# Four places of a fused graph network kernel: layer norm coefficients shared between VectorE and GpSimd, an earlier bank signal, and another order at the end of the score stage

## The chip, the cores and the metric

One NeuronCore of a Trainium2 chip runs the whole program in a single launch. The metric is the device time of that launch in microseconds. Engines are named as the profile names them: PE (TensorE), DVE (VectorE), ACT (ScalarE), POOL (GpSimd) and SP (the queue that issues most DMAs).

## The reference, cut to what matters

The input x has 128 graphs of 128 nodes with 128 features. Four blocks follow one another, each of the form x = x + block(relu(layernorm(x))):

```python
h = jnp.maximum(_layernorm(x, axis=-1), 0.0)
x = x + L0(h, W, adj, bias)                  # diagonal, upper and lower part of adj, each with its own W
h = jnp.maximum(_layernorm(x, axis=-1), 0.0)
x = x + L1(h, adj, ...)                      # GCN: A_hat h W1 + b1, batchnorm, relu, W2 + b2, batchnorm
h = jnp.maximum(_layernorm(x, axis=-1), 0.0)
x = x + L2(h, adj, ...)                      # two graph convolutions, then LSTMs over windows of 1 to 4 nodes
h = jnp.maximum(_layernorm(x, axis=-1), 0.0)
x = x + L3(h, src, dst, ...)                 # attention over 256 edges: scores, softmax per source node, sum
```

All arithmetic is fp32, or fp32 split into a high and a low part for the faster pass of PE.

## The kernel before, in words

X stays in SBUF as 32 tiles of 4 graphs (128 partitions by 512 elements). Each stage runs over the tiles in 16 turns of two slots, s = 0 and 1. The program is written engine by engine, and every engine's order is the order of its instructions; semaphores tie the engines together. There are no planner and no due times around the change: an engine that waits holds back all that is written behind the wait.

**Layer norm coefficients.** DVE makes statistics of a tile with four `bn_stats` (`LayerNormTail.stats`, L126). Then POOL turns the six statistics of each graph into 1/std (`rstd`) and -mean/std (`nmr`) in five dependent groups (`batch`, L153 to L179): sum, difference, squares, a `pow` with exponent -0.5, and two products. It does so for both slots of a turn at once (128x8 operands). Only for the very first turn of the first stage it goes tile by tile (`coefficients_alone`, 128x4). ACT waits for these (`LayerNormTail.wait`) and normalises a tile with four activations (`normalise_tile`, L185).

**First stage** (`stage_first`). DVE's order at the start is: statistics of tile 0, the split of the adjacency, a copy of its diagonal, statistics of tile 1, the row sums (`degrees`), a memset, statistics of tiles 2 and 3 interleaved with the low parts of h for tiles 0 and 1 (`h_low`, L468), then the loop over turns. PE transposes h (L410), multiplies with the adjacency (L418 to L420, which wait for `h_low`) and then with the weights (L431 to L433). Dummy matmuls (`stay_awake`, L80) keep PE busy before that.

**GCN out part** (`stage_gcn_out`). DVE makes the batchnorm coefficients (L703 to L713), then four products for the signed projection (L783 to L789) and three for the value projection (L796 to L801), and after them gives the free signal of the two PSUM banks (`O_stored`, L807). ACT makes h2 from the coefficients (L755), and PE (L772, L774) waits for h2 and for the bank signal. In the loop DVE takes each tile out of the bank (L813) and makes statistics of it (L816).

**Convolution stage** (`stage_conv`). A step t does work for several tiles at once: the residual of tile t+4 (PE turns it over, L854; DVE adds it to X, L861, and makes its statistics, L126), the normalised tile t+1 on ACT, the products of tiles t to t-3 on PE (L979, L1002), each taken over by DVE (L1029, L1025, L1019) or ACT (L971, L962). The steps t = -4 to -1 are the head of the stage. `FILL` gives numbers of dummy matmuls in some steps. POOL makes the coefficients for two tiles at a time.

**Scores** (`Scores`, last turns i = 13, 14 and 15). Per turn PE transposes h (L1528), makes Q (L1541), V (L1547) and, from q split by ACT (L1503) and DVE (L1580), the edge sums (L1560, L1561). DVE makes M from these (L1593), POOL halves it (L1450), DVE sums it (L1459). The softmax of the first chunk of scores is spread over the last turns: `score_in` to `subtract_max` on DVE at the end of turn 13 (L1657 to L1670), the exponential on ACT in turn 14 in front of the normalisation of tile (15,0) (L1674), `turn_back` on PE between the two V products of turn 14 (L1684), `keep_exponential` on DVE (L1689), `sum_up` on PE in front of the edge sums of turn 14 (L1695), `invert` (L1701) and `weigh` (L1705) on DVE. The exponential's table is loaded at the end of turn 13 (L1679). `at.high`, `at.low`, `at.gather` and `at.weighted` (L1799, L1803, L1758, L1836) are the first steps of the attend stage behind it.

## Time and profile before

| | us |
|---|---|
| median of 3 runs | 1208.47 (1206.82 to 1209.98) |
| the profiled execution | 1208.81 |
| its span | 1207.0 |
| PE busy in the span | 1175.3 (97%) |
| DVE busy | 978.5 (81%) |
| ACT busy | 899.6 (75%) |
| POOL busy | 438.3 (36%) |

The span runs from the first to the last instruction of the core; 1.81 us of the execution lie outside it. PE is nearly always busy, so the time is read from the places where PE waits, or where its granted clock is lower than full: the timeline of each engine in such a stretch tells what was late, and the chain of work that ended last tells whether the wait was on the path. In a timeline the first column is the start in us, the second the duration from the first to the last of the instructions merged into the row, then engine, line, operation, output and inputs, and in brackets the engine's idle time before it and what ended it.

### The profile page before, as it was taken

How to read it: one execution, taken by the hardware profiler on the slowest of the kernel's cores; microseconds unless marked ns; L12 is line 12 of the kernel's file. 1: busy time of each engine (PE TensorE's matmuls, PEld its weight loads, DVE VectorE, ACT ScalarE, POOL GpSimd, SP SyncE). 2: the span in 40 equal slices, each digit the busy share in tenths (PEclk: the TensorE clock that was granted, in tenths of full speed). 3: DMA queues.
4: the chain of work that ended last, by engine and by line, in shares of the span. 5: the costliest groups of instructions: out<-in, count | busy, mean ns of one | idle time of the engine just before them, and what ended most of it. 6: DMA issues, size and time to landing. Idle time of an engine off the chain costs nothing.

```text
span 1207.0 us, 22297 instructions
## 1 busy us (share of the span) xinstructions
PE 1175.3 (97%) x7208; PEld 1018.0 (84%) x7208; DVE 978.5 (81%) x2005; ACT 899.6 (75%) x1729; POOL 438.3 (36%) x803
## 2 busy tenths in 40 slices
PE   8999999999999999999999999999999999989998
PEld 8999988864688886798878887898898899978997
DVE  5888859978788877988788878887787799978774
ACT  5767669968588878877787868776776688875554
POOL 5778747800277450000000000000000477757764
PEclk9999999999999999999999999999999999999999
DMA  8000000000311100000000000000300120001122
GB/s 326 1 2 2 2 1 0 1 1 0 113 71 63 67 36 1 1 2 1 1 1 1 2 0 2 1 1 1 140 2 1 37 105 2 2 1 53 70 76 82
DMA packets 14923, 38.21 MB, mean 32 GB/s; under 512 B 1904, under 2 KB 3952, under 8 KB 13808
## 3 DMA queue, kind: packets, MB, share of 16 engines
q1 hardware_dynamic: 14000, 36.60, 7.9%
q8 instruction: 50, 0.82, 0.3%
q10 hardware_dynamic: 832, 0.46, 0.1%
q14 instruction: 41, 0.34, 0.1%
HBM read 20.27 MB, written 16.78 MB: 31 GB/s over the span
## 4 chain that ended last, share of the span: by engine, by line
PE 67%; DVE 6%; ACT 3%; issue 1%; POOL 1%; POOLq 0%; DVEq 0%; ACTq 0%
PE psum L1241 7%; PE psum L979 7%; PE psum L1242 7%; PE psum L1240 7%; PE psum L1269 5%; PE psum L1265 4%; PE psum L1266 4%; PE psum L1541 2%; PE psum L1793 2%; PE psum L772 2%; PE psum L774 2%; PE psum L1758 2%; PE psum L1547 2%; PE psum L1002 2%; PE psum L1768 2%; ACT gates L1286 2%
## 5 line engine op out<-in xcount | busy, mean ns | idle before, releaser
L1286 ACT ACTIVATE gates<-psum,lstm_bias 128x512 f32<-128x512 f32 (+1 forms) x504 | 302.2, 637 | 99.2 <-PE psum L1269 86.9
L153 POOL TENSOR_TENSOR l2r_sum<-l2r_st 128x8 f32<-128x8 f32 x16 | 5.2, 322 | 500.8 <-DVE l2r_st L126 500.5
L185 ACT ACTIVATE l_h<-X,nmr,rstd 128x128 f32<-128x128 f32 (+1 forms) x392 | 160.6, 484 | 14.3 <-POOLq L179 14.3
L1241 PE MATMUL psum<-lstm_node_hi,Wih_lo 128*128 128x512 f32 (+1 forms) x408 | 148.3, 363 | 0.0
L1242 PE MATMUL psum<-lstm_node_lo,Wih_hi 128*128 128x512 f32 (+1 forms) x408 | 148.0, 363 | 0.0
L1240 PE MATMUL psum<-lstm_node_hi,Wih_hi 128*128 128x512 f32 (+1 forms) x408 | 148.0, 363 | 0.0
L1265 PE MATMUL psum<-lstm_hid_hi,Whh_hi 128*128 128x512 f32 (+1 forms) x288 | 104.1, 361 | 3.9 <-DVE lstm_hid_hi L1348 3.7
L1269 PE MATMUL psum<-lstm_hid_lo,Whh_hi 128*128 128x512 f32 (+1 forms) x288 | 107.3, 373 | 0.0
L1266 PE MATMUL psum<-lstm_hid_hi,Whh_lo 128*128 128x512 f32 (+1 forms) x288 | 103.0, 358 | 0.0
L1296 ACT ACTIVATE gates<-lstm_cell 128x512 f32<-128x512 f32 (+1 forms) x144 | 83.7, 581 | 20.9 <-DVE lstm_cell L1335 20.5
L1240 PEld LDWEIGHTS psum<-lstm_node_hi,Wih_hi 128*128 128x128 f32 x408 | 77.2, 189 | 10.8 <-ACT gates L1286 0.3
L1242 PEld LDWEIGHTS psum<-lstm_node_lo,Wih_hi 128*128 128x128 f32 x408 | 77.2, 189 | 10.2
L1241 PEld LDWEIGHTS psum<-lstm_node_hi,Wih_lo 128*128 128x128 f32 x408 | 77.2, 189 | 10.1
L1329 DVE TENSOR_TENSOR lstm_cell<-gates 128x512 f32<-128x512 f32 (+1 forms) x72 | 46.9, 651 | 30.1 <-ACT gates L1286 27.6
L1269 PEld LDWEIGHTS psum<-lstm_hid_lo,Whh_hi 128*128 128x128 f32 x288 | 54.1, 188 | 16.0 <-DVE lstm_hid_lo L1350 10.2
L1265 PEld LDWEIGHTS psum<-lstm_hid_hi,Whh_hi 128*128 128x128 f32 x288 | 54.2, 188 | 12.1 <-DVE lstm_hid_hi L1348 6.1
L1331 DVE TENSOR_TENSOR gates<-gates 128x512 f32<-128x512 f32 (+1 forms) x72 | 43.8, 608 | 25.1 <-ACT gates L1286 24.8
L1266 PEld LDWEIGHTS psum<-lstm_hid_hi,Whh_lo 128*128 128x128 f32 x288 | 54.4, 189 | 6.8
L1343 DVE TENSOR_TENSOR Y<-gates 128x512 f32<-128x512 f32 (+1 forms) x72 | 46.5, 646 | 13.7 <-ACT gates L1296 13.7
L755 ACT ACTIVATE l1b_h<-Y,l1b_coef 128x512 f32 (+1 forms) x64 | 48.5, 806 | 11.2 <-PE psum L774 9.1
L431 PE MATMUL psum<-W,l_z 128*128 128x128 f32 x256 | 50.3, 278 | 3.6 <-DVE l_z L540 3.0
L340 ACT ACTIVATE l_z<-psum 128x512 f32<-128x512 f32 x32 | 19.1, 597 | 42.3 <-PE psum L420 42.3
(279 smaller groups left out, 3449.7 us busy)
## 6 DMA issues: line engine op xcount, KB each, us to landing
x_spill<-X SPq DMA_DIRECT2D x32, 256.0 KB, 2.0
X<-x_spill SPq DMA_DIRECT2D x2, 4096.0 KB, 12.9
out<-X SPq DMA_DIRECT2D x32, 256.0 KB, 2.0
X<-in_x SPq DMA_DIRECT2D x6, 1024.0 KB, 15.3
X<-in_x SPq DMA_DIRECT2D x3, 512.0 KB, 7.8
w_raw<-in_WihT SPq DMA_DIRECT2D x1, 1024.0 KB, 5.3
w_raw<-in_WhhT SPq DMA_DIRECT2D x1, 1024.0 KB, 7.6
X<-in_x SPq DMA_DIRECT2D x2, 256.0 KB, 3.5
```

Of the source, the lines that this page charges most:

```text
L185: last = act.activation(h[:, j, :], k.X[:, bass.ds(b0, TB), :][:, j, :], ACT.Relu, bias=k.nmr[:, bass.ds(b0, TB)][:, j:j + 1], scale=k.rst ...
L431: pe.matmul(o, Z0[s][:, j, :], W0[:, 0, :], start=True, stop=False)
L755: act.activation(h2[s][:, c, :], Y[c][:, bass.ds((i * S + s) * TW, TW)], ACT.Relu, bias=coef[:, c, 1:2], scale=coef[:, c, 0:1]).then_inc(h ...
L979: last = pe.matmul(ps[:, j * P:(j + 1) * P], lhs[:, j, :], rhs, start=True, stop=True)
L1240: pe.matmul(out, hi, x_high, start=True, stop=False)
L1241: pe.matmul(out, lo, x_high, start=False, stop=False)
L1242: last = pe.matmul(out, hi, x_low, start=False, stop=it.step == 0)
L1265: pe.matmul(out, hi, h_high, start=False, stop=False)
L1266: pe.matmul(out, lo, h_high, start=False, stop=False)
L1269: pe.matmul(out, hi, h_low, start=False, stop=True).then_inc(done[s], 1)
L1286: act.activation(gate_of(it, g), k.bank[4 * s + g][:, 0:it.N], ACT.Tanh if g == GATE_G else ACT.Sigmoid, bias=k.lstm_bias[:, it.p - 1, g:g ...
L1296: act.activation(gate_of(it, GATE_G), cell[it.slot][:, 0:it.N], ACT.Tanh).then_inc(tanh_ready[it.slot], 1)
```

## The change

1. Layer norm coefficients of the first two turns, in the first stage (`x_ln`) and at the head of the convolution stage (the residual's `ln`), are made by DVE and POOL together: `aggregate` on DVE (a `bn_aggr` for each graph, and + EPS), `root` on POOL (the `pow` alone), `shift` on DVE (-mean * rstd). The first turn goes tile by tile, the second both tiles at once. Later turns are made as before.
2. In the GCN out part the bank signal stands ahead of the coefficients and the projections.
3. In the convolution stage the numbers of dummy matmuls in the head change, and DVE makes the residual update behind the other work in steps 0 to 2.
4. In the last turns of the scores the softmax steps move to later places, and the normalisation of tile (15,1) goes from ACT to POOL.

```diff
+    def aggregate(self, dve, turn, s=0):
+        before, first, width, _ = self.shared_rows(turn, s)
+        for slot in [s] if turn == 0 else range(self.S):
+            dve.wait_ge(self.stats_ready[slot], turn + 1)
+        dve.sem_inc(self.dve_tally, 1)
+        for j in range(width):
+            last = dve.bn_aggr(self.mv[:, j, :], self.st6[:, first + j:first + j + 1, :])
+        last.then_inc(self.quick, 1)
+        dve.wait_ge(self.quick, before + 1)
+        if turn or s == self.S - 1:
+            dve.sem_inc(self.stats_free[0], 1)
+        dve.tensor_scalar(self.mv[:, 0:width, 1], self.mv[:, 0:width, 1], EPS, None, ALU.add).then_inc(self.quick, 1)
+
+    def root(self, pool, turn, s=0):
+        before, _, width, rows = self.shared_rows(turn, s)
+        pool.wait_ge(self.quick, before + 2)
+        pool.tensor_tensor(out=self.k.rstd[:, rows], in0=self.mv[:, 0:width, 1], in1=self.k.ln_const["-half"][:, 0:width],
+                           op=ALU.pow).then_inc(self.quick, 1)
+
+    def shift(self, dve, turn, s=0):
+        before, _, width, rows = self.shared_rows(turn, s)
+        dve.wait_ge(self.quick, before + 3)
+        dve.scalar_tensor_tensor(self.k.nmr[:, rows], self.mv[:, 0:width, 0], -1.0, self.k.rstd[:, rows],
+                                 ALU.mult, ALU.mult).then_inc(self.quick, 1)
+        dve.wait_ge(self.quick, before + 4)
+        dve.sem_inc(self.ready[0], 1)
...
             x_stats(0, [0])
+            x_ln.aggregate(dve, 0, 0)
             dve.wait_ge(masks, 2)
...
             dve.tensor_copy(diag_bc[:, :], spare[:, 0:P]).then_inc(diag_done, 1)
+            x_ln.shift(dve, 0, 0)
             x_stats(0, [1])
+            x_ln.aggregate(dve, 0, 1)
             degrees()
+            x_ln.shift(dve, 0, 1)
+            h_low(0, 0)
+            x_stats(1)
+            x_ln.aggregate(dve, 1)
+            h_low(0, 1)
             dve.memset(cont[:, :], 0.0).then_inc(cleared, 1)
-            x_stats(1, [0])
-            h_low(0, 0)
-            x_stats(1, [1])
-            h_low(0, 1)
...
+                if i == 0:
+                    x_ln.shift(dve, 1)
                 if i + AHEAD < n_it:
                     x_stats(i + AHEAD)
...
+        for s in range(S):
+            dve.sem_inc(O_stored[s], 1)
         coef_dve(dve)
         signed_projection()
         value_projection()
-        for s in range(S):
-            dve.sem_inc(O_stored[s], 1)
...
-    FILL = {-2: 3, -1: 4, 0: 18, 1: 1}
+    FILL = {-2: 5, -1: 6, 1: 3}
...
+        def first_coefficients(dve, t):
+            ln = res.ln
+            if 0 < t <= S:
+                ln.shift(dve, 0, t - 1)
+            if 0 <= t < S:
+                ln.aggregate(dve, 0, t)
+            if t == 2 * S - 1:
+                ln.aggregate(dve, 1)
...
-            if there(t + RES):
+            late = isinstance(t, int) and 0 <= t < 3
+            if there(t + RES) and not late:
                 res.update(dve, i + RES // S, [s])
+            if isinstance(t, int) and t < 0:
+                first_coefficients(dve, t + RES)
...
                 dve.tensor_copy(Z[:, :, :], as_tile(psZ)).then_inc(Z_done, 1)
+            if there(t + RES) and late:
+                res.update(dve, i + RES // S, [s])
+            if isinstance(t, int) and t == 0:
+                res.ln.shift(dve, 1)
...
+    def normalise_on_pool(self, pool, i, s):
+        k, h = self.k, self.h[s]
+        self.ln.wait(pool, s, i)
+        pool.wait_ge(self.R["Tp"][s], i)
+        for j in range(TB):
+            b = (i * self.S + s) * TB + j
+            last = pool.tensor_scalar(h[:, j, :], k.X[:, b, :], k.rstd[:, b:b + 1], k.nmr[:, b:b + 1], ALU.mult, ALU.add)
+        last.then_inc(self.normed, 1)
+        pool.wait_ge(self.normed, 1)
+        pool.tensor_scalar(h[:, :, :], h[:, :, :], 0.0, 0.0, ALU.max, ALU.add).then_inc(self.R["h"][s], 1)
...
                 if i == n_it - 1 and s == 0:
                     at.low(pool, 2)
+            if i == n_it - 3:
+                self.normalise_on_pool(pool, n_it - 1, 1)
...
-            if i == n_it - 2:
-                at.sm.exponential(act, 0)
+            if i == n_it - 1:
+                for t in range(2):
+                    at.high(act, t)
...
-            if i + 1 < n_it:
+            if i + 2 < n_it:
                 self.normalise(act, i + 1, 1)
-            if i == n_it - 3:
+            if i == n_it - 2:
                 at.sm.load_exponential(act)
-            if i == n_it - 2:
-                for t in range(2):
-                    at.high(act, t)
+                at.sm.exponential(act, 0)
...
+            if i == n_it - 1:
+                at.sm.turn_back(pe, 0)
...
-                if i == n_it - 2 and s == S - 1:
-                    at.sm.turn_back(pe, 0)
+                if i == n_it - 1 and s == 0:
+                    at.sm.sum_up(pe, 0)
...
-            if i == n_it - 2:
-                at.sm.sum_up(pe, 0)
...
-            if i and i != n_it - 2:
+            if i and i < n_it - 2:
                 self.sum_heads(dve, i - 1)
...
-            if i == n_it - 2:
-                at.sm.keep_exponential(dve, 0)
+            if i == n_it - 1:
+                at.sm.invert(dve, 0)
+                at.sm.weigh(dve, 0)
+            if i >= n_it - 2:
                 self.sum_heads(dve, i - 1)
-                at.sm.invert(dve, 0)
...
             if i == n_it - 2:
-                at.sm.weigh(dve, 0)
+                at.sm.keep_exponential(dve, 0)
```

In the last turns this gives the following orders. DVE, turn 14: low parts of q, `sum_heads` of turn 13, M, `keep_exponential`; turn 15: low parts of q, `invert`, `weigh`, `sum_heads` of turn 14, M of slot 0, `weighted(0)`, M of slot 1, `weighted(1)`. ACT, turn 14: both hT, normalisation of (15,0), q, V, table load, exponential; turn 15: both hT, `high(0)`, `high(1)`, q, V. PE, turn 15: both transposes, `turn_back`, Q, `sum_up`, V, edge sums. POOL: the normalisation of (15,1) stands behind the halving of turn 13, and ahead of that of turn 14.

## Rows read from the trace of the kernel before

**Rows 1.** The page: its first line, and the chain that ended last by engine
```profile
span 1207.0 us, 22297 instructions
...
PE 67%; DVE 6%; ACT 3%; issue 1%; POOL 1%; POOLq 0%; DVEq 0%; ACTq 0%
```

**Rows 2.** Timeline of the first stage's start, 0 to 40 us, several engines
```profile
5.38 0.86 DVE L126 BATCH_NORM_STATS2 x_st<-X 128x6 f32<-128x128 f32 x4
...
8.49 1.07 POOL L153 TENSOR_TENSOR x_m<-x_m,ln_const 128x4 f32<-128x4 f32 x1 [0.18 <-POOL x_m L153]
...
9.89 0.20 POOL L153 TENSOR_TENSOR nmr<-x_sum,x_m 128x4 f32<-128x4 f32 x1
10.17 1.65 ACT L185 ACTIVATE l_h<-X,nmr,rstd 128x128 f32<-128x128 f32 x4 [6.17 <-POOLq L179]
...
16.28 0.69 DVE L468 TENSOR_TENSOR l_h_lo<-l_h,l_h_hi 128x512 fp32r<-128x512 f32 x1 [2.29 <-ACT l_h_hi L325]
...
17.03 0.19 PEld L418 LDWEIGHTS psum<-l_A_hi,l_h_hi 128*128 128x128 f32 x1 [0.25 <-DVE l_h_lo L468]
```

**Rows 3.** Timeline of DVE at the head of the out part: small instructions
```profile
253.47 0.15 DVE L705 TENSOR_SCALAR bn_mv<-bn_mv 128x1 f32<-128x1 f32 x1
253.54 1.01 DVE L703 BATCH_NORM_AGGREGATE bn_mv<-bn 128x2 f32<-128x192 f32 x1
```

**Rows 4.** Head of the out part: timelines of ACT and PE, and one window
```profile
255.31 2.93 ACT L755 ACTIVATE l1b_h<-Y,l1b_coef 128x512 f32<-128x512 f32 x4 [2.09 <-DVE l1b_coef L713]
...
257.79 1.20 PE L772 MATMUL psum<-l1b_h,W2T 128*128 128x512 f32 x2 [2.41 <-DVEq L807]
...
263.02 1.02 PE L772 MATMUL psum<-l1b_h,W2T 128*128 128x512 f32 x2
...
260.00:262.00 2.00, 2.00 (x3) 0.67 (x2) 0.90 (x2) 1.16 (x2) 0.00 (x0) 0.50 0.00 0
```

**Rows 5.** Timelines at the head of the convolution stage: DVE, ACT, POOL, PE
```profile
323.18 0.87 DVE L126 BATCH_NORM_STATS2 l1r_st<-X 128x6 f32<-128x128 f32 x4 [0.18 <-DVE X L861]
...
328.51 1.65 ACT L185 ACTIVATE l_h<-X,nmr,rstd 128x128 f32<-128x128 f32 x4 [5.49 <-POOLq L179]
...
330.72 1.65 POOL L153 TENSOR_TENSOR l1r_m<-l1r_m,ln_const 128x8 f32<-128x8 f32 x1 [0.18 <-POOL l1r_m L153]
...
333.05 1.65 ACT L185 ACTIVATE l_h<-X,nmr,rstd 128x128 f32<-128x128 f32 x4
...
335.27 1.16 PE L979 MATMUL psum<-Wg,l_G 128*128 128x128 f32 x8 [0.67 <-ACT l_G L971]
```

**Rows 6.** Timelines of the last turns of the scores: ACT, PE and DVE
```profile
1064.95 1.28 ACT L1679 ACT_TABLE_LOAD   x1
1066.25 0.20 ACT L1679 ACTIVATE sm_unread<-zero 128x1 f32<-128x1 f32 x1
...
1066.99 2.05 PE L1541 MATMUL psum<-Wqv,l_hT 128*128 128x128 f32 x16 [1.32 <-ACT l_hT L1496]
...
1068.81 0.42 DVE L1670 TENSOR_TENSOR sm_r<-sm_r,sm_w 128x256 f32<-128x256 f32 x1
...
1073.41 1.16 PE L1695 MATMUL psum<-scores,same 128*128 128x128 f32 x8 [2.33 <-DVE scores L1689]
...
1077.31 0.63 PE L1561 MATMUL psum<-l_q_lo,PT 128*128 128x512 f32 x1
...
1074.61 1.76 DVE L1701 RECIPROCAL sm_m<-psum 128x256 f32<-128x256 f32 x1
...
1076.28 2.42 DVE L1593 SCALAR_TENSOR_TENSOR l_M<-psum,a_sign 128x512 f32<-128x512 f32 x4
...
1087.80 1.28 DVE L1836 TENSOR_TENSOR at_w<-psum,scores 128x512 f32<-128x512 f32 x2
```

**Rows 7.** Groups by line and shape, POOL: busy time and mean of one
```profile
L609 POOL TENSOR_SCALAR l_h<-l_h 128x256 f32<-128x256 f32 x26 | 27.8, 1068 | 5.4 <-POOL l_h L604 5.4
...
L604 POOL TENSOR_SCALAR l_h<-X,rstd,nmr 128x128 f32<-128x128 f32 x52 | 23.0, 453 | 9.0 <-PE psum L659 6.9
```

More of the change, by code:

```diff
@@ L88, with __init__ @@
     GROUPS = 5
-    def __init__(self, k, ctx, name, S, nb=TB, per=2, at=None, first_alone=False, places=1):
-        self.first_alone, self.places = first_alone, places
+    def __init__(self, k, ctx, name, S, nb=TB, per=2, at=None, first_alone=False, places=1, shared=0):
+        self.first_alone, self.places, self.shared = first_alone, places, shared
         top = at
@@ L106, in __init__ @@
         self.stats_free, self.ready = (each(S // per, lambda q: k.sem(f"{name}_{n}{q}")) for n in ("stfree", "coef"))
+        if shared:
+            self.mv = place("mv", [P, per * nb, 2])
+            self.quick = k.sem(f"{name}_quick")
         self.step, self.tally, self.dve_tally = (k.sem(f"{name}_{n}") for n in ("step", "tally", "dve_tally"))
@@ L116, in wait @@
     def wait(self, eng, s, turn):
-        eng.wait_ge(self.ready[s // self.per], turn + 1 + (self.first_alone and (turn > 0 or s == 1)))
+        eng.wait_ge(self.ready[s // self.per], turn + 1 + (self.first_alone and (not isinstance(turn, int) or turn > 0 or s == 1)))
     def stats(self, dve, xt, s, turn):
@@ L127, in stats, with shared_rows @@
         last.then_inc(self.stats_ready[s], 1)
+    def shared_rows(self, turn, s):
+        n = s if turn == 0 else turn + 1
+        first, width = (s * self.nb, self.nb) if turn == 0 else (0, self.per * self.nb)
+        return 4 * n, first, width, slice(turn * self.per * self.nb + first, turn * self.per * self.nb + first + width)
+    def aggregate(self, dve, turn, s=0):
[22 more added lines that the diff above has]
+        dve.sem_inc(self.ready[0], 1)
     def coefficients(self, pool, turn):
@@ L147, in batch @@
         late = self.first_alone and (alone is None or alone == 1)
-        base = (turn * self.batches + q + late) * self.GROUPS
+        base = (turn * self.batches + q + late - (self.shared and self.shared + 1)) * self.GROUPS
         rows = bass.ds((turn * self.batches + q) * whole + first, width)
@@ L252, in stage_first @@
     spare = psO[0]
-    x_ln, ln = LayerNormTail(k, ctx, "x", S, first_alone=True), k.l0_ln
+    x_ln, ln = LayerNormTail(k, ctx, "x", S, first_alone=True, shared=2), k.l0_ln
     SCALE, SPREAD, READ, KEYS, WIDE, RANK, PERM, SORTED, ROUND, ADJ, SUM, TURN, SHARE = 0, 2, 2, 3, 4, 5, 6, 8, 9, 10, 11, 12, 13
@@ L295, in _ @@
             for s in range(S):
-                x_ln.coefficients_alone(pool, s)
+                x_ln.root(pool, 0, s)
             pool.wait_ge(deg, 4)
             pool.tensor_tensor(out=dinv[:, :], in0=rs[:, 3:4], in1=k.ln_const["-half"][:, 0:1], op=ALU.pow).then_inc(dinv_p, 1)
-            x_ln.coefficients(pool, 1)
+            x_ln.root(pool, 1)
             pool.iota(order_row[:, :], [[1, E]], base=0, channel_multiplier=0, allow_small_or_imprecise_dtypes=True).then_inc(iotas, 1)
@@ L737, in stage_gcn_out @@
     tally, logged, signed = hidden.tally, sem("l1b_logged"), sem("l1b_signed")
-    joined, stats_done = sem("l1b_joined"), sem("l1b_stats")
+    stats_done = sem("l1b_stats")
     unread = sb("l1b_unread", [P, 1])
@@ L795, in value_projection @@
             dve.wait_ge(signed, 4)
-            dve.tensor_tensor(W[:, 0:P], e.Wqv[:, 0:P], e.a_sign[:, :], ALU.mult).then_inc(joined, 1)
-            dve.wait_ge(joined, 1)
+            dve.tensor_tensor(W[:, 0:P], e.Wqv[:, 0:P], e.a_sign[:, :], ALU.mult).then_inc(signed, 1)
+            dve.wait_ge(signed, 5)
             dve.tensor_reduce(W[:, P:P + H], W[:, 0:P].rearrange("p (x d) -> p x d", x=H), mybir.AxisListType.X,
-                              ALU.add).then_inc(joined, 1)
-            dve.wait_ge(joined, 2)
-            dve.tensor_copy(W[:, 0:P], e.Wqv[:, P:2 * P]).then_inc(joined, 1)
+                              ALU.add).then_inc(signed, 1)
+            dve.wait_ge(signed, 6)
+            dve.tensor_copy(W[:, 0:P], e.Wqv[:, P:2 * P]).then_inc(signed, 1)
+        for s in range(S):
+            dve.sem_inc(O_stored[s], 1)
         coef_dve(dve)
@@ L843, in __init__ @@
         self.o_ready, self.R_ready, self.updated = (each(S, lambda s: k.sem(f"{name}_{n}{s}")) for n in ("o", "R", "upd"))
-        self.ln = LayerNormTail(k, ctx, name, S)
+        self.ln = LayerNormTail(k, ctx, name, S, first_alone=True, shared=2)
     def fetch(self, act, s, source):
@@ L927, in on_pool @@
         AHEAD = 2
-        for i in range(AHEAD):
-            res.coefficients(pool, i)
+        for s in range(S):
+            res.ln.root(pool, 0, s)
+        res.ln.root(pool, 1)
         for n, W in enumerate((k.Wih, k.Whh)):
@@ L1407, in __init__ @@
         self.R = {n: each(S, lambda s: k.sem(f"l3_{n}{s}")) for n in names}
+        self.normed = k.sem("l3_normed")
         self.n_it = k.B // TB // S
```

## The prediction

> **What bounds the kernel now.** I read the chain of work that ended last first: PE holds 67% of the span on it [rows 1], so a saving counts where PE waits for something late, or runs at a low clock. The changed lines lie in four such places, each read from the engines' timelines.
>
> *Start.* POOL's last product starts at 9.89, ACT normalises tile 0 at 10.17, though its statistics began at 5.38 [rows 2]. PE starts the products of tile 1 at 17.03, released by `h_low`, which ran from 16.28 [rows 2].
>
> *Out part.* ACT begins h2 at 255.31, PE only at 257.79, after 2.41 us of waiting for the bank signal behind DVE's projections [rows 4]. Its granted clock then falls to 0.50 (1.2 of 2.4 GHz) between 260 and 262 [rows 4]; the third tile starts at 263.02.
>
> *Convolution head.* ACT gets its first coefficients at 328.51 and those of turn 1 for 333.05; PE enters its steady order at 335.27, released by ACT's G [rows 5].
>
> *Score end.* PE waits 1.32 us for hT, which stands behind the table load, and 2.33 us at `sum_up`; after that each edge pass takes 0.63 us, at a lower clock [rows 6].
>
> **The change, part by part.** Times are those of the profiled execution.
>
> *Small instructions on DVE.* No row shows a `bn_aggr` of six numbers. Two small DVE instructions without a dependence started 0.07 us apart [rows 3]; the aggregate of 192 numbers took 1.01 us [rows 3]; a `bn_stats` of 128 took 0.20 per instruction (0.87 for four, the last with its latency [rows 5]). If the 1.01 is a fixed 0.15 [rows 3] and the rest by length, six numbers add 0.03. I take 0.10 each; the ends are 0.07 and, should the price be all fixed, 1.0. One `aggregate` of four then takes about 0.15 (wait and semaphore, as the 0.18 in front of the statistics [rows 5]) + 0.40 + 0.15 + 0.10 = 0.8, one of eight 1.2, a `shift` with its waits 0.3.
>
> *Small instructions by the skill.* The Trainium skill ("VectorE: DVE Perf Modes", the TRN2 errata) says many small tiles each pay a fixed latency, measured at some 150 cycles, 0.156 us by its clock. The rows' 0.07 speaks against it. By it the 32 aggregates would cost 32 x 0.056 = 1.8 us more than in my sum, which is inside rival A.
>
> *Start.* Statistics of tile 0 end at 6.24; aggregate to 7.1; `root` 1.07 [rows 2] to 8.2; split and diagonal copy lie beside it; `shift`, and ACT at 8.55 instead of 10.17. But DVE now carries everything: statistics of tile 1 from 8.55, aggregate, `degrees` (1.3), `shift` at 11.5, `h_low(0,0)` at 11.75, statistics of two tiles (1.6), aggregate of eight (1.2), `h_low(0,1)` at about 15.1 instead of 16.28 [rows 2]. PE takes the products of tile 1 1.2 us earlier, and the turn-1 coefficients (root to 16.95, shift at 17.75) stay ahead of ACT, which is at its Z copies until 18.6. The memset now stands in front of the first Z0 and costs nothing: Z0 is done at 16.6, and PE asks for it at 17.3. **Gain 1.2.** PE's dummies end at 11.2 and hold nothing up.
>
> *Out part.* PE starts when the first half of h2 is there, 255.31 + 0.85 = 256.17, 1.62 earlier [rows 4]. DVE's projections (to 257.95) are then beside PE: the first tile leaves the bank from 258.0, and PE needs that bank for the third tile only at 256.17 + 4 x 0.86 = 259.6. PE idled 2.41 us before the fall of the clock, and will idle 0.8, so I take the clock as kept: third tile 259.6 instead of 263.02 [rows 4]. **Gain 3.4**; with the clock still falling, 1.7. From there the loop is PE's, 1.72 a tile, with ACT and DVE waiting for it.
>
> *Convolution head.* DVE's row of work per tile is 1.65 us (0.60 add, 0.17 wait, 0.87 statistics [rows 5]). Written out from 321.53: aggregate of tile 0 to 323.1; update 1; `shift` near 324.9; ACT normalises tile 0 at 325.2, 3.3 us earlier than 328.51 [rows 5]. Aggregate to 325.8; update 2; `shift` 327.6; update 3 to 329.5; aggregate of eight to 330.8. Only then comes DVE's copy Z(0), at 330.7 (before: 331.4, waiting for PE). Behind it stand update 4 (to 333.0) and `shift` of turn 1, though `root` (1.65 [rows 5]) is over by 332.5. ACT gets turn 1 at 333.3, against 333.05 [rows 5]. G follows that normalisation in ACT's order, so PE's steady order starts at 335.5, against 335.27 [rows 5]. The early tiles gain nothing: DVE is late next. **Loss 0.2**, from a gain of 0.3 (0.07 each) to a loss of 1.8 (0.20 each). Dropping 18 dummies costs nothing in itself, but PE now idles 1 to 2 us four times between 322 and 335; should the clock fall there, as it did after 2.4 us [rows 4], up to 1.7 more.
>
> *Score end.* ACT's hT of turn 14 no longer waits for the table load (1.28 [rows 6]): Q starts at 65.9 (of 10xx, as all here) instead of 66.99 [rows 6]. DVE ends `subtract_max` at 69.2 [rows 6], makes q_lo to 70.45, and the edge sums run 69.9 to 71.8 at the full clock (eight passes of 0.23), not held by `sum_up` at 73.41 [rows 6]. The next tile: (15,0) is ready at 67.9; (15,1) is POOL's. POOL ends the halving at 68.2; four scalings of 0.45, less overlap, and a 128x512 clamp at twice 1.07 [rows 7] give 4.2, so 72.4. PE transposes it to 72.95; hT 73.75. The exponential, now behind table load and V, ends at 72.25 and hides in that wait. `turn_back` 72.95, Q 73.2 to 75.1, `sum_up` to 76.0, V to 77.8; M of turn 14 71.6 to 74.05 (2.42 [rows 6]), `keep_exponential` 74.4. DVE then: q_lo 75.4 to 76.6, `invert` 1.76 [rows 6] to 78.4, `weigh`, `sum_heads` to 80.05, M 0 to 81.2, `weighted(0)` 82.4 (gathered by 80.15), M 1 83.6, `weighted(1)` at 83.6 instead of 87.80 [rows 6]. POOL's halving of slot 1 shifts as much, so what hangs on it (the low parts) too. **Gain 4.2**, of it 1.6 for the clock. Bounds: a slower clamp (3 us for 2.1) leaves 3.2; `sum_heads` of turn 14 ahead of M is on the path, and with everything else a little late it is 2.8; at best 4.8.
>
> *The load by the skill.* The activation after the table load started 1.30 us after it, that is at once [rows 6]. The Trainium skill ("ScalarE: Activation LUTs", What ACT_TABLE_LOAD costs) adds a drain of 1.38 us to the load's 1.28, by which the exponential would end at 73.6, in front of hT(15,0); this trace does not show the drain.
>
> Sum: 1.2 + 3.4 - 0.2 + 4.2 = 8.6. Profiled execution 1208.81 (span 1207.0 [rows 1] and 1.8 outside); less 8.6 is 1200.2. The median of the runs, 1208.47, lies 0.3 lower, well inside their spread, so I leave 1200.2.
>
> **The rivals.**
> A. *An aggregate costs as much as a `bn_stats`*, 0.20. For: both reduce over the free dimension; against: six numbers, not 128. Twice 16 aggregates lie on DVE's path, in the start and in the convolution head: 32 x 0.10 = 3.2 less, 1203.4. Chance 0.15.
> B. *The clock falls in the convolution head or still in the out part.* For: the idle stretches above; against: none reaches 2.3 us. 1.7 less, 1201.9. Chance 0.17.
> C. *ACT stays shut behind the load for as long again as the load*, 1.28 [rows 6]: the exponential ends at 73.5, hT(15,0) and (15,1) move from 73.05 and 73.75 to 74.1 and 74.7, and Q, with all behind it, 1.0 later: 1201.2. Against: in the trace the activation follows the load at once [rows 6]. Chance 0.03.
> D. *The other side: the aggregate's 1.0 us is mostly fixed.* Place: the same 32 instructions; price 32 x (a - 0.10) for a price a each; it eats the gain of 8.6 at a = 0.37. With a = 0.5 the time is 1200.2 + 12.8 = 1213.0. The only row of the operation shows 1.01 [rows 3] and does not split it; against: all other DVE instructions there scale with length. Chance 0.04.
> E. *The score end gives nothing*, because POOL's normalisation runs against DVE's traffic and comes 4 us late, as the halving and the low parts behind it: 1204.4, and with A's price on top within 0.3% of before. Chance 0.06 for the first, of it half within 0.3%.
>
> **How the numbers follow.** The forecast has what is left, 0.55. The bound of 0.3%, about what a measurement of this kernel can tell from no change, is 3.6 us, so faster means under 1204.9. Faster: 0.55 + 0.13 + 0.17 + 0.03 + 0.03 = 0.91; the same: a part of A that meets B, and half of E, 0.05; slower: D, 0.04. The range goes from 1197.6 (aggregates at 0.07, 1.0 less; the score end at its best, 0.6; and the ten waits around aggregates and shifts at 0.1 less each, 1.0) to 1204.0, which takes in A, B and C; about 0.15 is left out.
>
> **What would show it.** `bn_aggr` rows starting 0.10 apart; ACT's first normalisation at 8.5; `h_low(0,1)` at 15.1; in the out part no wait for DVE's queue, a clock of 1.00 in all its windows, and 1.72 us between its tiles from the first; in the convolution head ACT's first normalisation 3.7 us behind the residual's first statistics (7.0 before), but PE's steady order no earlier, with PE waiting for DVE's Z(0) and ACT's G; in the score end no `sum_up` wait, POOL's clamp near 2.1, the clock at 1.00, and `weighted(1)` 4.2 us earlier against the first transposes of turn 13. A `bn_aggr` start distance over 0.3, or a clock of 0.50 in two places, makes the prediction wrong.

## The result, and the profile after

| | before | after |
|---|---|---|
| median of the runs | 1208.47 (6 runs, 1206.82 to 1210.74) | 1201.97 (6 runs, 1201.10 to 1203.02) |
| the profiled execution, its span | 1208.81, 1207.0 | 1202.42, 1200.6 |

The ratio is 0.9949, 95% interval 0.9938 to 0.9960, which is 4.8 to 7.5 us. The medians are 6.5 us apart, where 8.6 was forecast (1201.97 for 1200.2, inside the range of 1197.6 to 1204.0). Two of the 64 later runs of the kernel before (1656 and 2360 us) and one of only_start (1294 us) were in a slow state and are left out of everything below. In the trace three of the four terms came out near their size and one was more than five times too small; a loss that no term held came on top, and half of one gain turned out to belong to some executions and not to the kernel. I compare the two traces by the **lead**: the start of an instruction before, less the start of the same instruction after. It is 1.47 us where the first stage has ended, 4.71 in the GCN out part, 3.57 in the convolution stage, 2.25 at the end of the LSTM, 6.51 at `weighted(1)` and 6.4 at the end.

First the page, its first line and the chain by engine [rows 1]:

```profile
span 1200.6 us, 22233 instructions
...
PE 63%; DVE 6%; ACT 2%; issue 1%; POOL 1%; POOLq 0%; DVEq 0%; ACTq 0%
```

PE's share of the chain is lower than before (67%), and the average does not show where 6 us went, the stretches do. The start, several engines [rows 2]:

```profile
6.13 0.38 DVE L148 BATCH_NORM_AGGREGATE x_mv<-x_st 128x2 f32<-128x6 f32 x4
...
8.13 1.65 ACT L225 ACTIVATE l_h<-X,nmr,rstd 128x128 f32<-128x128 f32 x4 [4.13 <-DVEq L167]
...
13.86 0.65 DVE L148 BATCH_NORM_AGGREGATE x_mv<-x_st 128x2 f32<-128x6 f32 x8
...
15.10 0.69 DVE L508 TENSOR_TENSOR l_h_lo<-l_h,l_h_hi 128x512 fp32r<-128x512 f32 x1 [0.27 <-issue]
...
15.85 0.39 PE L458 MATMUL psum<-l_A_hi,l_h_hi 128*128 128x256 f32 x1 [0.64 <-DVE l_h_lo L508]
```

ACT normalises tile 0 2.0 us earlier, but PE's products of tile 1 come only 1.2 earlier (17.03 to 15.85), because `h_low(0,1)` stands behind all that DVE now carries. Of both, 0.25 is not the change's: the execution of before that is compared began its first DVE instruction, which waits for a DMA, at 5.17, this one at 4.92. Eight aggregates took 0.65: they start 0.07 apart.

The out part, PE's timeline [rows 4]:

```profile
254.78 1.12 PE L818 MATMUL psum<-l1b_h,W2T 128*128 128x512 f32 x2 [0.88 <-ACT l1b_h L801]
...
258.31 1.02 PE L818 MATMUL psum<-l1b_h,W2T 128*128 128x512 f32 x2
```

and one window of it (us; then busy time and count of PE, PEld, DVE, ACT and POOL; the granted clock of PE; DMA share and GB/s):

```profile
258.00:262.00 4.00, 4.00 (x11) 1.79 (x10) 3.46 (x5) 3.46 (x5) 0.00 (x0) 1.00 0.00 0
```

The wait is for ACT's h2 and no longer for DVE's queue, the clock stays at 1.00, and the third tile comes 4.71 us earlier than 263.02, which is 3.24 more than the lead on entry.

The head of the convolution stage, DVE, ACT and PE in order of time [rows 5]:

```profile
325.24 0.58 DVE L148 BATCH_NORM_AGGREGATE l1r_mv<-l1r_st 128x2 f32<-128x6 f32 x7 [0.25 <-issue]
...
328.59 1.65 ACT L225 ACTIVATE l_h<-X,nmr,rstd 128x128 f32<-128x128 f32 x4 [3.35 <-DVEq L167]
...
330.81 1.16 PE L1026 MATMUL psum<-Wg,l_G 128*128 128x128 f32 x8 [1.58 <-ACT l_G L1018]
...
334.36 0.68 DVE L907 TENSOR_TENSOR X<-psum,X 128x512 f32<-128x512 f32 x1
...
335.23 0.87 DVE L129 BATCH_NORM_STATS2 l1r_st<-X 128x6 f32<-128x128 f32 x4 [0.18 <-DVE X L907]
...
336.02 0.67 DVE L907 TENSOR_TENSOR X<-psum,X 128x512 f32<-128x512 f32 x1
...
336.87 0.87 DVE L129 BATCH_NORM_STATS2 l1r_st<-X 128x6 f32<-128x128 f32 x4 [0.18 <-DVE X L907]
...
337.66 0.67 DVE L1080 TENSOR_TENSOR l_V<-psum,rows 128x512 f32<-128x512 f32 x1
...
338.46 1.15 PE L1026 MATMUL psum<-adjT,l_V 128*128 128x128 f32 x8 [0.33 <-DVE l_V L1080]
...
342.83 1.06 PE L1026 MATMUL psum<-adjT,l_V 128*128 128x128 f32 x8
```

The first G product is 4.46 us earlier than 335.27, so 0.25 of the lead is gone, as forecast (0.2). But then updates 6 and 7 stand together on DVE (334.36 to 337.7), V2(1) is behind both, and PE's steps take 4.47 and 4.37 us (333.99, 338.46, 342.83) where the undisturbed ones take 3.98. In the first of the two PE waits 0.33 for V2(1); in the second G, which ACT makes from DVE's next output, is late. Those two steps cost another 0.88.

The LSTM's head, two windows of the changed kernel:

```profile
478.00:482.00 4.00, 2.22 (x8) 1.23 (x7) 3.79 (x7) 2.88 (x6) 0.00 (x0) 0.95 0.00 0
482.00:485.00 3.00, 3.00 (x8) 2.35 (x8) 2.28 (x4) 1.87 (x3) 0.00 (x0) 0.50 0.00 0
```

and the same work in the kernel before, 3.6 us later:

```profile
480.00:484.00 4.00, 2.40 (x11) 1.63 (x9) 3.75 (x7) 3.74 (x8) 0.00 (x0) 1.00 0.00 0
484.00:488.00 4.00, 3.82 (x15) 2.85 (x16) 3.90 (x8) 2.95 (x5) 0.00 (x0) 1.00 0.00 0
```

The code is the same in both, and so are PE's waits ahead of it (0.44, 0.65, 1.05 and 1.78 us, within 0.01 in both traces). After, the clock is 0.50 (1.2 of 2.4 GHz) from 482 to 485, and the lead falls from 3.59 to 2.03. This stretch is in no term of the prediction.

The score end, several engines in order of time [rows 6]:

```profile
1063.65 2.05 PE L1623 MATMUL psum<-Wqv,l_hT 128*128 128x128 f32 x16 [0.25 <-ACT l_hT L1577]
...
1065.98 2.27 POOL L1541 TENSOR_SCALAR l_h<-X,rstd,nmr 128x128 f32<-128x128 f32 x4
...
1068.23 1.28 ACT L1760 ACT_TABLE_LOAD   x1
1068.34 1.93 POOL L1544 TENSOR_SCALAR l_h<-l_h 128x512 f32<-128x512 f32 x1
...
1069.53 0.20 ACT L1760 ACTIVATE sm_unread<-zero 128x1 f32<-128x1 f32 x1
...
1072.95 1.06 PE L1776 MATMUL psum<-scores,same 128*128 128x128 f32 x8
...
1074.39 1.75 DVE L1782 RECIPROCAL sm_m<-psum 128x256 f32<-128x256 f32 x1
...
1081.29 1.27 DVE L1917 TENSOR_TENSOR at_w<-psum,scores 128x512 f32<-128x512 f32 x2
```

`sum_up` waits for nothing, and `weighted(1)` leads by 6.51 against 2.24 at the first transposes of turn 13: 4.27 gained.

### The profile page after: what moved, and what is told of

The parts are those of the page before. It is cut to its first block, busy times and chain, and to the rows that moved or that the text cites. A ratio compares the mean times of both kernels' runs of the same rounds, so it can differ in the third digit from the quotient of the medians.

```text
span 1200.6 us, 22233 instructions
## 1 busy us (share of the span) xinstructions
PE 1171.2 (98%) x7184; PEld 1015.1 (85%) x7184; DVE 982.8 (82%) x2049; ACT 898.0 (75%) x1725; POOL 433.0 (36%) x764
## 4 chain that ended last, share of the span: by engine, by line
PE 63%; DVE 6%; ACT 2%; issue 1%; POOL 1%; POOLq 0%; DVEq 0%; ACTq 0%
PE psum L1306 7%; PE psum L1305 7%; PE psum L1307 7%; PE psum L1026 7%; PE psum L1334 5%; PE psum L1330 4%; PE psum L1331 4%; PE psum L1874 2%; PE psum L1623 2%; PE psum L1839 2%; PE psum L1049 2%; PE psum L1629 2%; PE psum L1849 2%; PE psum L1640 1%; PE psum L1860 1%; ACT gates L1351 1%
```

## The experiments

All runs together, in us. "Groups" are the runs of a kernel sorted by time; they lie in clumps, and the column gives how many lie near which value. "Falls" are the stretches at a clock of 0.50 in the profiled execution, the last instants of the program left aside. The kernel before ran beside each of the three sets of experiments; its groups are those 62 runs, its median and its falls those of the start. Its medians beside the sets are 1208.25 (the four parts), 1208.39 (conv_as_before to conv_staggered) and 1207.99 (the last four rows), and it is with these that a run's median is compared below.

| kernel | median | ratio to before (95%) | groups | falls |
|---|---|---|---|---|
| before | 1208.47 | | 28 at 1206.8, 27 at 1208.4, 7 at 1209.9 | out part, score end |
| after | 1201.97 | 0.9949 (0.9938 to 0.9960) | 3 at 1201.4, 3 at 1202.8 | LSTM head |
| only_start | 1208.02 | 1.0003 (0.9993 to 1.0014) | 4 at 1206.4, 3 at 1208.1, 2 at 1209.3 | score end |
| only_signal | 1206.24 | 0.9988 (0.9979 to 0.9998) | 5 at 1205.4, 5 at 1206.8 | score end |
| only_conv | 1209.46 | 1.0015 (1.0006 to 1.0025) | 1 at 1208.0, 5 at 1209.4, 4 at 1211.1 | out part, LSTM head, score end |
| only_score | 1202.80 | 0.9961 (0.9950 to 0.9971) | 5 at 1202.7, 3 at 1204.4, 1 at 1205.8 | out part |
| conv_as_before | 1201.54 | 0.9947 (0.9931 to 0.9964) | 2 at 1200.7, 2 at 1202.3 | LSTM head |
| lstm_filled | 1202.92 | 0.9960 (0.9946 to 0.9974) | 5 at 1202.8 | none |
| late_signal_filled | 1210.27 | 1.0022 (1.0013 to 1.0032) | 6 at 1210.0, 4 at 1211.6 | score end |
| conv_staggered | 1202.15 | 0.9951 (0.9934 to 0.9967) | 1 at 1200.4, 3 at 1202.2 | LSTM head |
| late_signal_filled_again | 1207.23 | 0.9998 (0.9988 to 1.0007) | 5 at 1206.5, 5 at 1208.0 | score end |
| sum_wait_filled | 1206.16 | 0.9991 (0.9980 to 1.0002) | 5 at 1205.3, 3 at 1207.0, 2 at 1208.4 | out part |
| last_tile_on_scalar | 1203.38 | 0.9961 (0.9946 to 0.9975) | 2 at 1202.1, 3 at 1203.7 | LSTM head |
| staggered_and_filled | 1200.35 | 0.9940 (0.9922 to 0.9958) | 4 at 1200.4 | none |

**The groups are the clock.** They are 1.3 to 1.7 us apart, and each profiled execution belongs to the group that its number of falls says: before (1208.81, two falls) to the second; only_start (1206.44), only_signal (1205.24) and late_signal_filled_again (1206.46), with the fall of the score end alone, to the first; only_conv (1211.18, three falls) to the third; only_score (1204.57) and sum_wait_filled (1206.94), which have no fall at the score end but one in the out part, to the second. The mean granted clock, which is given for every run, agrees: over the 62 runs of the kernel before it is 0.9985, 0.9969 and 0.9960 in the first, second and third group. So does the number of groups. The kernels with the long wait in the out part and the LSTM's head as before have three (before, only_start, only_conv, only_score, sum_wait_filled: 16 of 100 runs in the third), those without the long wait have two (none of 49 runs in a third), and those that also have the LSTM's wait filled have one. So the same program, run again, meets the fall in one of these two places or does not. Parts are therefore compared group by group, beside the ratio of all runs.

### One part of the change at a time

**only_start.** The kernel before with the first stage as changed:

```diff
-                x_ln.coefficients_alone(pool, s)
+                x_ln.root(pool, 0, s)
...
-            x_ln.coefficients(pool, 1)
+            x_ln.root(pool, 1)
```

> The kernel before with the start alone changed (coefficients of turns 0 and 1 of the first stage by DVE and POOL together). My theory: the start's term stands by itself, 1.2 to 1.5 us faster than before (the whole change led by 1.47 at the end of the start). If the lead were used up by a later wait of the same stage, it would be 0. Rival: the price of the aggregates is paid later; then under 1.0.

Its lead over before is 1.19 us from 120 us on. But every kernel here whose first stage is as before leads that execution too at 250 us, by 0.2 to 0.3, so that execution was itself late and the part is worth 0.9 to 1.0 in the trace. Nor does that last: between 790 and 970 us, where the code is as before, the lead falls from 3.04 to 2.57, in two steps that the changed kernel's trace does not have. What they are is open. The groups moved by 0.3 to 0.6, and the ratio shows nothing. Its out part had no fall, with the late signal and a wait as before, and the lead went from 1.19 to 2.89 there without any edit. The window there:

```profile
257.00:261.00 4.00, 4.00 (x11) 1.72 (x10) 1.99 (x3) 2.13 (x4) 0.00 (x0) 1.00 0.00 0
```

Against the 0.50 of [rows 4] this is the first row that shows the fall there as a matter of chance. That the start's lead reaches the end in full was not shown; the runs bear out about half of it.

**only_signal.**

```diff
+        for s in range(S):
+            dve.sem_inc(O_stored[s], 1)
         coef_dve(dve)
         signed_projection()
         value_projection()
-        for s in range(S):
-            dve.sem_inc(O_stored[s], 1)
```

> The kernel before with the bank signal alone moved to the head of the out part. My theory: 3.2 to 3.4 us faster, of it 1.6 of wait and 1.6 to 1.8 because TensorE's clock stays at 1.00 between 258 and 263. Rival: the clock falls all the same, then 1.6 to 1.7.

In the trace the lead goes from 0.28 to 1.81 at the first product (the wait, 1.5) and to 3.51 at the third tile (the clock, 1.7). In the runs the groups moved by 1.4 and 1.6, which is the wait alone, the third group is gone, and the median is 2.0 lower. The two executions that were traced said 3.2.

**only_conv.**

```diff
-    FILL = {-2: 3, -1: 4, 0: 18, 1: 1}
+    FILL = {-2: 5, -1: 6, 1: 3}
...
+            late = isinstance(t, int) and 0 <= t < 3
+            if there(t + RES) and not late:
```

> The kernel before with the convolution head alone changed. By the prediction 0.2 us slower (from 0.3 faster to 1.8 slower). By what the changed kernel's trace shows (updates 6 and 7 stand back to back on DVE, and PE waits for DVE's V2 and for ACT's G after them) 1.1 us slower. If both are wrong and the losses belong to the other parts, no difference.

The lead falls from 0.26 to -0.52: 0.8 us lost, with the same two long steps of PE (338.08, 342.56, 346.92; 4.48 and 4.36 us). The groups moved by 0.9 to 1.3, and 9 of 10 runs are in the second and third; why falls are more frequent in this kernel is not settled. No fall is inside the convolution head in its profiled execution.

**only_score.** All of part 4, and nothing else.

```diff
-            if i == n_it - 3:
+            if i == n_it - 2:
                 at.sm.load_exponential(act)
...
+            if i == n_it - 3:
+                self.normalise_on_pool(pool, n_it - 1, 1)
```

> The kernel before with the score end alone changed. My theory: 4.2 us faster (4.27 was the lead won there in the whole change). Rival: part of that lead came from the earlier parts or from the phase of the clock; then under 3.5.

The lead goes from 0.24 to 4.39 at the end, 4.15; the groups moved by 4.0 to 4.1. This term stands by itself, in the trace and in the runs.

### Undoing and repairing the convolution head

**conv_as_before.** The changed kernel with the part undone:

```diff
-        self.ln = LayerNormTail(k, ctx, name, S, first_alone=True, shared=2)
+        self.ln = LayerNormTail(k, ctx, name, S)
...
-    FILL = {-2: 5, -1: 6, 1: 3}
+    FILL = {-2: 3, -1: 4, 0: 18, 1: 1}
...
-            late = isinstance(t, int) and 0 <= t < 3
-            if there(t + RES) and not late:
+            if there(t + RES):
```

> The changed kernel with its convolution head undone (as in the kernel before). My theory now: the new convolution head loses 0.8 to 1.1 us where DVE's updates 6 and 7 stand back to back, so this one is 0.8 to 1.1 us faster than the changed kernel. The prediction's 0.2 would be the difference if the loss seen were the execution's own.

Behind the head it leads the changed kernel by 0.84 after trailing by 0.30 at its entry: 1.14 gained, and PE's steps are 3.98 us from the first, in PE's timeline:

```profile
334.04 1.06 PE L1025 MATMUL psum<-adjT,l_V 128*128 128x128 f32 x8
...
338.02 1.06 PE L1025 MATMUL psum<-adjT,l_V 128*128 128x128 f32 x8
...
341.99 0.28 PE L1025 MATMUL psum<-adjT,l_V 128*128 128x128 f32 x1
```

Of this 1.14 only 0.4 is left at the end of that execution: it loses 0.2 near 795 us and 0.3 near 965, as only_start's did, and 0.2 in smaller steps, all where the code is the same. The groups are 0.5 to 0.7 lower than the changed kernel's; the two medians (1201.54 and 1201.97, four and six runs) do not tell the two apart. So the third part of the change costs about 1 us in the head itself and 0.6 by the groups, and gains nothing. only_conv, the same part alone, says 0.8 and 0.9 to 1.3.

**conv_staggered.** The changed kernel with updates 5 and 6 each moved forward on DVE:

```diff
-            late = isinstance(t, int) and 0 <= t < 3
-            if there(t + RES) and not late:
-                res.update(dve, i + RES // S, [s])
+            late = {0: 3, 1: 2}.get(t, 0) if isinstance(t, int) else 0
+            def update(n):
+                if there(t + RES) and late == n:
+                    res.update(dve, i + RES // S, [s])
+            update(0)
...
+            update(2)
             if there(t):
                 dve.wait_ge(Zp_done, t + 1)
                 dve.tensor_copy(Z[:, :, :], as_tile(psZ)).then_inc(Z_done, 1)
-            if there(t + RES) and late:
-                res.update(dve, i + RES // S, [s])
+            update(3)
```

> The changed kernel with the residual's updates 5 and 6 moved forward on DVE: update 5 stands ahead of the copy Z(1) instead of behind it, update 6 ahead of V2(0). Written out: Z(1) ends at 331.6, needed by PE at 331.8; V2(0) ends at 333.9, needed at 334.0; G(1) comes 0.4 us late; updates 6 and 7 no longer stand together. My theory: 0.4 to 0.7 us faster than the changed kernel. If DVE's whole work between 328.6 and 338 is what bounds it, no difference; slower by up to 0.5 if one of the two deadlines is missed.

DVE and PE there:

```profile
331.05 0.68 DVE L1095 COPY l_Z<-psum 128x512 f32<-128x512 f32 x1
...
333.29 0.67 DVE L1084 TENSOR_TENSOR l_V<-psum,rows 128x512 f32<-128x512 f32 x1
...
334.21 1.06 PE L1026 MATMUL psum<-adjT,l_V 128*128 128x128 f32 x8
...
335.28 1.16 PE L1026 MATMUL psum<-Wg,l_G 128*128 128x128 f32 x8
...
338.46 1.06 PE L1026 MATMUL psum<-adjT,l_V 128*128 128x128 f32 x8
...
342.44 0.83 PE L1026 MATMUL psum<-adjT,l_V 128*128 128x128 f32 x6
```

Both deadlines are met, and the first step is 4.25 us instead of 4.47, the second 3.98 instead of 4.37: 0.6 us, from a lead of -0.2 to 0.4. The runs alone do not tell it from the changed kernel (medians 1202.15 and 1201.97), since three of its four had the LSTM's fall.

### The clock

**lstm_filled.** The changed kernel with dummies in the LSTM head's fourth wait:

```diff
             if it.step:
                 h_high, h_low = columns(it, hid_hi[s]), columns(it, hid_lo[s])
+                if it.n == GROUP // TB + 1 and s == 0:
+                    stay_awake(pe, k, k.bank[4 + GATE_F], 18)
```

> The changed kernel with 18 dummy products on PE in the fourth wait of the LSTM's head (1.78 us before the first products with Whh). My theory: TensorE's clock falls after that row of waits in some executions and not in others, and each fall costs 1.4 to 1.6 us; filled, it falls in none, so all runs lie within 0.5 us of the changed kernel's fastest, 1201.1, and the median is 0.6 to 1.4 us below 1201.97. Rival: the fall has another cause, then the runs still stand in two groups about 1.4 us apart.

PE's timeline:

```profile
478.67 4.18 PE L80 MATMUL psum<-ones,ident 128*128 128x128 f32 x36
482.61 0.48 PE L1332 MATMUL psum<-lstm_hid_hi,Whh_hi 128*128 128x512 f32 x1
```

I had sized the dummies wrongly: each is two matmul records, 0.22 us together, so 18 fill 3.9 us, and the products with Whh start 2.0 late (480.59 before that). The median is worse, but the runs form one group, 0.43 wide: the fall is gone.

**late_signal_filled** and **late_signal_filled_again.** The kernel before with more dummies ahead of the out part's loop, 45 and then, with the right size, 28:

```diff
-        stay_awake(pe, k, k.bank[7], 18)
+        stay_awake(pe, k, k.bank[7], 28)
```

> The kernel before with its late bank signal, but 45 dummy products in place of 18, so that PE's wait of 2.41 us at the head of the out part is filled. The first product cannot start earlier, so the 1.6 us of the wait stay; only the clock can gain. My theory: the fall there happens in a part of the executions, so the median is 0.4 to 1.0 us faster than before, and no run has a fall between 258 and 262. By the prediction, which took the fall as given, 1.6 to 1.8 us faster. If the clock falls for another reason than the idle PE, no difference.

> The kernel before with its late bank signal and 28 dummy products in place of 18: each takes 0.22 us of PE in the records, so ten more fill 2.2 of the 2.41 us of wait (the 45 of the run before filled 5.9 and were late themselves). My theory: the start of the products stays, and the fall of the clock there, which comes in a part of the executions only, is gone: fastest runs as of the kernel before (1206.8), median 0.3 to 1.0 us below it. By the prediction, which took the fall as given, 1.6 to 1.8 us faster in all runs. If idle PE is not what makes the clock fall there, no difference.

The 45 delayed the first product to 260.93, from 257.79, and cost 1.9 at the median, so they say nothing of what the fall costs; but their ten runs, too, stand in only two groups. The 28 leave the wait at 0.17 us, by PE's timeline,

```profile
257.52 1.12 PE L772 MATMUL psum<-l1b_h,W2T 128*128 128x512 f32 x2 [0.17 <-DVEq L807]
```

and the clock is kept, by the window:

```profile
256.00:262.00 6.00, 5.83 (x24) 3.25 (x23) 3.55 (x9) 4.14 (x6) 0.00 (x0) 1.00 0.00 0
```

Against the profiled execution of before the lead goes from 0.26 to 1.96, so the fall costs 1.7 where it comes. In the runs the third group has gone (0 of 10, where the kernel before had 3 of 19 in the same set; too few to tell by themselves), the fastest group has not moved, and the median is 0.8 lower; the ratio's interval, 0.9988 to 1.0007 (at most 1.45 us faster), holds no change and leaves out the 1.6 to 1.8 of the prediction.

**sum_wait_filled.** The kernel before with dummies in the 2.33 us ahead of `sum_up`:

```diff
             if i == n_it - 2:
+                stay_awake(pe, k, k.bank[0], 9)
                 at.sm.sum_up(pe, 0)
```

> The kernel before with nine dummy products (2.0 us) in the 2.33 us that PE waits ahead of sum_up in turn 14. No wait ends earlier; only the clock can gain. My theory: the fall there is in every execution of the kernel before, and the low clock's eight edge passes cost 1.6 us, so all runs shift by 1.5 to 1.7 us: fastest 1205.2, median 1.6 lower than before. If the fall comes from the 1.32 us wait further ahead, it stays, and there is no difference.

PE's timeline at `sum_up`, and the window behind it; the last two lines are the kernel before, where this work lies 0.7 us later:

```profile
1072.67 1.16 PE L1696 MATMUL psum<-scores,same 128*128 128x128 f32 x8 [0.33 <-DVE scores L1690]
```
```profile
1074.00:1078.00 4.00, 3.67 (x24) 2.94 (x22) 4.00 (x6) 2.20 (x5) 1.16 (x1) 1.00 0.00 0
```
```profile
1074.00:1076.00 2.00, 2.00 (x10) 1.64 (x9) 1.94 (x2) 1.86 (x5) 0.00 (x0) 0.62 0.00 0
1076.00:1078.00 2.00, 2.00 (x7) 1.47 (x6) 2.00 (x4) 0.00 (x0) 0.42 (x1) 0.52 0.00 0
```

The low clock is gone. The eight edge passes and what is between them take 1.96 us (1073.59 to 1075.55) instead of 3.42. The lead goes from 0.74 to 1.77, so of the 1.5 saved on PE 1.0 arrives at the end; the groups moved by 1.3 to 1.5. The ratio's interval, 0.9980 to 1.0002, does not by itself tell this from no change; the shift of all three groups does. So idle PE makes the fall here, and nearly all runs of the kernel before have it, the fastest group too, since even that one moved. One of the 19 beside this set, at 1205.76 and 0.8 below its group, may be a run without it.

### The last tile, and the best version

**last_tile_on_scalar.** The changed kernel without the normalisation on POOL:

```diff
-            if i == n_it - 3:
-                self.normalise_on_pool(pool, n_it - 1, 1)
...
-            if i + 2 < n_it:
+            if i + 1 < n_it:
                 self.normalise(act, i + 1, 1)
```

> The changed kernel with the normalisation of the last tile (15,1) on ACT, ahead of the table load, instead of POOL. Written out: ACT normalises at 1068.2 to 1069.9, loads to 1071.15, the exponential ends at 1071.7, hT(15,0) starts at 1071.7 instead of 1070.32. My theory: 1.3 to 1.4 us slower than the changed kernel. Rival: ACT's hT was to wait for something else anyway, then under 0.5. With the longer wait of PE the clock may fall too, then up to 3.0.

ACT's timeline:

```profile
1070.14 1.28 ACT L1758 ACT_TABLE_LOAD   x1
...
1071.85 1.07 ACT L1575 ACTIVATE l_hT<-psum 128x512 f32<-128x512 f32 x2
```

It trails the changed kernel by 0.38 before this point and by 1.41 after it: 1.0 us, and 0.7 to 0.9 by the groups. The mechanism is as written, the size a quarter smaller: hT starts 1.53 later, 0.38 of which that execution had already lost. So about a quarter of the score end's gain is the move to POOL.

**staggered_and_filled.** conv_staggered with seven dummies (1.5 us) in the LSTM head, as in lstm_filled.

> The changed kernel with updates 5 and 6 moved forward (as in conv_staggered, which led the changed kernel by 0.6 us behind the convolution head) and seven dummy products (1.5 us) in the LSTM head's fourth wait, which this time end before the wait does. My theory: one group of runs near 1200.4 to 1200.8, median 1.2 to 1.6 us below the changed kernel's 1201.97. Rival: seven do not keep the clock up, then two groups, 1200.5 and 1202.1.

The LSTM head, PE's timeline and one window:

```profile
478.11 1.72 PE L80 MATMUL psum<-ones,ident 128*128 128x128 f32 x14
480.05 0.50 PE L1336 MATMUL psum<-lstm_hid_hi,Whh_hi 128*128 128x512 f32 x1 [0.22 <-DVE lstm_hid_hi L1419]
```
```profile
482.00:486.00 4.00, 4.00 (x19) 3.23 (x19) 3.47 (x6) 3.92 (x8) 0.00 (x0) 1.00 0.00 0
```

The lead over the changed kernel goes from -0.08 to 0.53 in the convolution head and to 2.11 in the LSTM's. All four runs lie within 0.22 us, at 1200.35, below both kernels; the ratio to before is 0.9940. In the two kernels with filled LSTM waits none of 9 runs has an extra fall. In the seven other kernels whose out part has no long wait but whose LSTM head is as before (only_signal, late_signal_filled, late_signal_filled_again, after, conv_as_before, conv_staggered, last_tile_on_scalar), 25 of 49 are in the slower group.

## Why the prediction was right, and where it was wrong

**Small instructions on DVE: mis-sized, on the safe side.** I took 0.10 us an aggregate, between 0.07 and 1.0. Four took 0.38 and eight 0.65, a distance of 0.07: the lower end. Rivals A and D are out. The Trainium skill's 150 cycles fixed for each small tile ("VectorE: DVE Perf Modes", the TRN2 errata), by estimate 0.156 us at its clock, is twice what these rows show as the distance between independent instructions; as the time of one alone it fits them (0.17 for the 128x4 `+ EPS`).

**Start: the mechanism held, and the size in the trace.** Forecast 1.2, `h_low(0,1)` at 15.1 (it was 15.10), ACT at 8.5 (8.13). That the time agrees to the hundredth is luck: on the scale of the compared execution, 0.25 later, it is 15.35, and the aggregates were shorter than taken. The trace gives 1.2 for the whole change once that 0.25 is taken off, 0.9 to 1.0 for the part alone; the runs of the part alone show 0.3 to 0.6.

**Out part: right in the trace (3.24 for 3.4), wrong as a forecast of the runs.** The wait was to give 1.62 and gave 1.5, in the trace and in the groups. The failed step is "with the clock still falling, 1.7": I treated the fall as something that the kernel before has and the new one may or may not have. It comes there in a part of the executions only, as only_start's window at 1.00 and the groups show. Of the runs of the kernels with that wait 16 in 100 are in the third group, which has this fall and the LSTM's; as the LSTM's comes in half of the runs, the out part's comes in about a third, by estimate, if neither depends on the other. Weighed so, the 1.8 taken for the clock would have been some tenths.

**Convolution head: the failed term, -0.2 for -1.1.** The entry was worked out well: PE's G product lost 0.25. The working ended there ("PE's steady order starts at 335.5"). It did not follow the late updates to the step at which they stop being late. DVE makes update 6 behind Z(2) and update 7 ahead of V2(1), so V2(1) waits for both, 3.3 us of work, and PE for V2(1). conv_as_before gives back 1.14 at this place, conv_staggered, which spreads the change-over, 0.6 of it. The smaller number of dummies did not let the clock fall inside this head (1.00 in every profiled window), so this place of rival B did not come.

**LSTM head: not in the sum.** The traces differ by 1.56 us there, by the clock alone. In the five profiled executions that have this fall it costs 1.55 to 1.58. Not the change but the execution decides it: half of the runs with the same code have it (25 of 49), none of 9 with the wait filled. Rival B had the right mechanism and nearly the right size (1.7), but in two other places; that its time, 1201.9, is the measured one is luck.

**Score end: right (4.2 forecast, 4.27 and 4.15 measured).** The order of arrival was as worked, against the same mark: Q of turn 14 1.1 earlier (1.1 forecast), `sum_up` without a wait, POOL done at 1070.27, that is 72.5 on the old scale (72.4). POOL's four scalings took 2.27 where 4 x 0.45 were taken, the clamp 1.93 where twice 1.07 were: the errors cancel. Rival E is out. The clock's share is smaller than my 1.6: sum_wait_filled gives 1.0 in the trace and 1.3 to 1.5 in the groups. Rival C is out too: the activation stands at 1069.53, directly behind 1068.23 + 1.28, and the exponential behind it at 1069.64. The drain of 1.38 us of the Trainium skill ("ScalarE: Activation LUTs", What ACT_TABLE_LOAD costs) is not in this trace.

**The sum.** Lead by lead: 1.5 + 3.2 - 1.1 - 1.3 + 4.2 = 6.5 (the 1.3 being the LSTM's fall, 1.56, less 0.2 that came back up to turn 13; small steps of either sign between the marks make up the rest). Against 8.6 the two misses, 0.9 in the convolution head and 1.3 in the clock, are the whole difference. That is a comparison of two executions. The fastest group moved by 5.4 (1206.8 to 1201.4), and the mean of the six runs of the changed kernel, 1202.1, is 5.8 below that of the 62 of the kernel before, 1207.8; of the 6.5 between the medians, then, some tenths are the draw of six runs each. Group against group the LSTM's fall drops out, and the failed terms are the convolution head and the out part's clock: 8.6 less 0.9 and less 1.7 is 6.0, against 5.4 measured. What is left is about what the start loses on its way to the end in only_start.

## What to carry to other kernels

Where work is moved behind other work for the first few steps of a pipeline, follow it to the step at which the old order comes back: two steps' worth stands together there, and that is where the loss is; spread the change-over over several steps. One profiled execution shows one throw of the clock: before counting a low-clock stretch as something that an edit removes, look whether the kernel's runs fall into groups as far apart as that stretch is worth, and fill the idle wait ahead of it with a few dummies of known length, fewer than the wait holds.

## What I had not expected of the hardware

- Equal programs run in groups 1.3 to 1.7 us apart: 28, 27 and 7 of 62 runs of the kernel before. From one group to the next there is one more stretch at a clock of 0.50, behind a wait of 2.41 us in the out part or behind the row of 0.44, 0.65, 1.05 and 1.78 in the LSTM's head. The same wait of 2.41 brought the fall in four profiled executions and not in a fifth. The wait of 2.33 us at the score end, which follows one of 1.32, brought the fall in all six profiled executions that had it.
- A filler of 7 dummies in a wait of 1.78 us, leaving 0.22, removed the LSTM's fall in all four runs.
- The aggregate of six numbers starts every 0.07 us, the statistics of 128 every 0.20 (0.87 for four), and the aggregate of 192 took 1.02; alone it took 0.18. Nearly all of the long one's price goes by its length.
